# Message aggregation in three fp32r terms behind adjacency transposes and state parts, and the first norm's output of chunks 1 to 3 by ACT

## The reference

```python
x_conv = relu(h + x)                       # two convolutions, the second with 17 taps
s = x @ w_se.T + b_se                      # three position values of a node
A = exp(-dist(s, s)) * adj                 # (512, 512), weighed adjacency
msg = relu(x @ w_msg.T + b_msg)            # (512, 128)
x_nmp = einsum('nm,md->nd', A, msg)        # message aggregation
gi = concat(x_conv, x_nmp) @ w_ih.T + b_ih # gates of the inputs: r, z, n
gh = x @ w_hh.T + b_hh                     # gates of the state: r, z, n
r, z = sigmoid(gi_r + gh_r), sigmoid(gi_z + gh_z)
y = (1 - z) * tanh(gi_n + r * gh_n) + z * x
```

## Time and profile before

| | |
|---|---|
| median of 3 runs | 583.18 us (582.69 to 584.78) |
| profiled execution | 584.18 us, its span 582.4 us |
| PE busy | 560.3 us, 96% of the span |
| PE weight loads | 479.4 us, 82% |
| DVE | 476.7 us, 82% |
| ACT | 341.6 us, 59% |
| POOL | 120.8 us, 21% |
| mean granted TensorE clock | 0.988 |

### The profile page before, as it was taken

One profiled execution on the slowest core, in us unless ns is written; L12 is line 12 of the kernel. 1 busy time (PEld: TensorE's weight loads), 2 busy tenths in 40 slices (PEclk: granted clock), 3 DMA queues, 4 the chain that ended last, 5 costly groups with the idle time before them and its releaser, 6 DMA issues.

```text
span 582.4 us, 11740 instructions
## 1 busy us (share of the span) xinstructions
PE 560.3 (96%) x3583; PEld 479.4 (82%) x3583; DVE 476.7 (82%) x1798; ACT 341.6 (59%) x713; POOL 120.8 (21%) x143
## 2 busy tenths in 40 slices
PE   6888999999999999999999999999999999999894
PEld 6767897978888797979798888979797978889684
DVE  3898777888888887888888888888888988888665
ACT  2325555575675756665756667565667566575442
POOL 3311120213122130302121211203021213122110
PEclk9989999999999999999999999999999999999998
DMA  7890050030201103030303021020303030000000
GB/s 192 277 301 4 2 191 7 2 111 2 88 22 45 64 0 109 0 109 0 109 0 109 0 52 57 17 92 0 109 0 109 0 109 1 19 2 19 1 19 18
DMA packets 33300, 34.46 MB, mean 59 GB/s; under 512 B 1663, under 2 KB 22531, under 8 KB 33146
## 3 DMA queue, kind: packets, MB, share of 16 engines
q1 hardware_dynamic: 32986, 34.01, 18.6%
q10 hardware_dynamic: 288, 0.13, 0.1%
HBM read 29.74 MB, written 4.39 MB: 59 GB/s over the span
## 4 chain that ended last, share of the span: by engine, by line
PE 85%; DVE 1%; ACT 0%; issue 0%; POOLq 0%; POOL 0%; DVEq 0%
PE bank L260 14%; PE bank L262 14%; PE bank L261 13%; PE bank L1774 9%; PE pair L260 6%; PE pair L262 6%; PE pair L261 6%; PE bank L1608 4%; PE bank L1619 3%; PE bank L1710 2%; PE pair L1766 2%; PE pair L1698 2%; PE bank L1673 1%; PE bank L1716 1%; PE pair L1725 1%
## 5 line engine op out<-in xcount | busy, mean ns | idle before, releaser
L1147 POOL TENSOR_TENSOR rs<-ve,neg_half 128x4 f32<-128x4 f32 (+1 forms) x60 | 57.1, 952 | 279.0 <-DVE ve L1336 246.2
L260 PE MATMUL bank<-cd_hi,w_hi 128*128 128x256 f32 x272 | 77.5, 285 | 0.0
L261 PE MATMUL bank<-cd_lo,w_hi 128*128 128x256 f32 x272 | 76.7, 282 | 0.0
L262 PE MATMUL bank<-cd_hi,w_lo 128*128 128x256 f32 x272 | 76.5, 281 | 0.0
L1774 PE MATMUL bank<-P,msg 128*128 128x512 f32 x128 | 57.5, 592 | 0.0
L260 PE MATMUL pair<-aT_hi,x_hi 128*128 128x512 f32 x128 | 52.9, 413 | 0.1
L260 PEld LDWEIGHTS bank<-cd_hi,w_hi 128*128 128x128 f32 x272 | 51.3, 189 | 1.6
L261 PEld LDWEIGHTS bank<-cd_lo,w_hi 128*128 128x128 f32 x272 | 51.4, 189 | 1.4
L262 PEld LDWEIGHTS bank<-cd_hi,w_lo 128*128 128x128 f32 x272 | 51.3, 189 | 0.0
L262 PE MATMUL pair<-aT_hi,x_lo 128*128 128x512 f32 x128 | 50.4, 394 | 0.0
L261 PE MATMUL pair<-aT_lo,x_hi 128*128 128x512 f32 x128 | 50.3, 393 | 0.0
(11 more groups left out here) (367 smaller groups left out, 1522.3 us busy)
## 6 DMA issues: line engine op xcount, KB each, us to landing
adj_nat<-in_adj_dram SPq DMA_DIRECT2D x16, 1024.0 KB, 6.2
x_nat<-in_x_dram SPq DMA_DIRECT2D x16, 256.0 KB, 2.9
xt<-in_x_dram SPq DMA_DIRECT2D x3, 1280.0 KB, 11.4
out_dram<-y_out SPq DMA_DIRECT2D x15, 256.0 KB, 2.2
hw<-in_L_gnn_W_dram SPq DMA_DIRECT2D x2, 640.0 KB, 6.5
xt<-in_L_gnn_conv_w_dram SPq DMA_DIRECT2D x1, 1088.0 KB, 5.8
aT<-in_adj_dram SPq DMA_DIRECT2D x5, 96.0 KB
nat_ih<-in_L_gnn_w_ih_dram SPq DMA_DIRECT2D x1, 384.0 KB, 5.1
```

What stands on the lines that cost most here:

```text
L260: nc.tensor.matmul(o, lh, rh, start=start, stop=False)
L261: nc.tensor.matmul(o, lh, rl, start=False, stop=False)
L262: return nc.tensor.matmul(o, ll, rh, start=False, stop=stop)
L1147: g.tensor_tensor(rs[i][:, 0:n], ve[i][:, 0:n], neg_half[:, 0:n], ALU.pow).then_inc(po_rs[i], 1)
```

## The change

N becomes three fp32r terms. For that ACT rounds each weighed chunk (`P_hi`, four of 128x512) and the messages (`msg_hi`), POOL subtracts the rests of the four chunks (`P_lo`), DVE the rest of the messages (`msg_lo`). N's twelve products stand behind T0, T1, the state's parts of the gates z and r, and T2; the gates are taken in the order convolution parts of z, r, n, then message parts of z, r, n. In the turns without `new` the n gate goes behind the next turn's x3T. On ACT the exponentials 2 and 3 and the roundings go ahead of `y_out`; DVE's statistics of layer 3 go ahead of `nmp_lo` and the adjacency rests, and `aT_lo` of chunk 3 ahead of the sum of the n gate. The first norm's output of chunks 1 to 3 is written by ACT as `x1 * rs + fall`, with `fall` made by one small DVE instruction.

```diff
@@ -1174,6 +1180,11 @@
                         pool.wait_ge(dv_ve[3], V(0) + h)
                         g.tensor_tensor(rs[3][:, 2 * h:2 * h + 2], ve[3][:, 2 * h:2 * h + 2], neg_half[:, 0:2], ALU.pow
                                         ).then_inc(po_rs[3], 1)
+                if cur:
+                    for mc in range(NC):
+                        wait(pool, ac_Phi[mc], V(1))
+                        wait(pool, pe_N, V(0))
+                        g.tensor_tensor(P_lo[:, mc, :], P[:, mc, :], f(P_hi[:, mc, :]), ALU.subtract).then_inc(po_Plo[mc], 1)
                 if nxt:
                     inverse_root(V, 2, 2)
...
+
+                def round_weighed(mc):
+                    wait(act, dv_P[mc], V(1))
+                    wait(act, pe_N, V(0))
+                    s.activation(P_hi[:, mc, :], P[:, mc, :], ACT.Identity).then_inc(ac_Phi[mc], 1)
 
                 if cur:
...
@@ -1238,15 +1254,26 @@
                     wait(act, pe_P1, V(0))
                     s.activation(cd_hi[:, :, :], cd[:, :, :], ACT.Identity).then_inc(ac_cdh, 1)
                     wait(act, dv_s, V(1))
-                    wait(act, pe_N, V(0))
+                    wait(act, dv_msglo, V(0))
                     s.activation(msg_v[1], ms_half(ms_banks(nxt)[1]), ACT.Relu).then_inc(ac_msx, 1)
                     s.activation(msg_v[0], ms_half(ms_banks(nxt)[0]), ACT.Relu).then_inc(ac_msg, 1)
+                if nxt:
+                    wait(act, dv_fall, V(1))
+                    wait(act, dv_y3, V(1))
+                    wait(act, dv_xs[NC - 1], V(1))
+                    for c in range(1, NC):
+                        last = s.activation(x2[:, c, :], x1[:, c, :], ACT.Identity, bias=fall[:, c - 1:c], scale=rs[0][:, c:c + 1])
+                    last.then_inc(ac_x1r, 1)
+                if cur:
                     wait(act, pe_LR, V(1))
                     if not prev:
                         act.wait_ge(po_LR0, 1)
                     wait(act, pe_D[NC - 1], V(0))
                     s.activation(LR[0:KD, 0, :], SQ_BANK[0:KD, :], ACT.Identity)
                     s.activation(LR[0:KD, 1, :], SQ_BANK[GR:GR + KD, :], ACT.Identity).then_inc(ac_LR, 1)
+                    wait(act, ac_msg, V(1))
+                    wait(act, pe_N, V(0))
+                    s.activation(msg_hi[:, :], msg[:, :], ACT.Identity).then_inc(ac_msghi, 1)
                 if nxt:
                     wait(act, dv_f, V(2))
...
                     exponential(1)
+                if cur:
+                    round_weighed(0)
+                if nxt:
+                    wait(act, dv_e, V(2))
+                    wait(act, dv_dq, V(1))
+                    s.activation(pef[:, 0, :], ef[:, 0, :], ACT.Exp, bias=c12[:, 0:1]).then_inc(ac_pe, 1)
+                if nxt:
+                    wait(act, pe_agg2, V(2))
+                    s.activation(agg_sb[:, :], AG_BANK[:, :], ACT.Identity).then_inc(ac_agg2, 1)
+                if cur:
+                    exponential(2)
+                    exponential(3)
+                    round_weighed(1)
+                    round_weighed(2)
+                    round_weighed(3)
                 if prev and cur:
                     wait(act, po_shift, V(0))
                     wait(act, o_out, outs)
@@ -1270,16 +1312,7 @@
                         last = s.activation(y_out[:, c, :], X_BANK[:, ch(c)], ACT.Identity, bias=shift[:, c:c + 1],
                                             scale=rs[3][:, c:c + 1])
                     last.then_inc(ac_out, 1)
-                if nxt:
-                    wait(act, dv_e, V(2))
-                    wait(act, dv_dq, V(1))
-                    s.activation(pef[:, 0, :], ef[:, 0, :], ACT.Exp, bias=c12[:, 0:1]).then_inc(ac_pe, 1)
-                if nxt:
-                    wait(act, pe_agg2, V(2))
-                    s.activation(agg_sb[:, :], AG_BANK[:, :], ACT.Identity).then_inc(ac_agg2, 1)
-                if cur:
-                    exponential(2)
-                    exponential(3)
+                if cur:
                     wait(act, dv_conv, V(1))
                     wait(act, pe_gn, V(0))
...
                     wait(dve, ac_E[mc], V(1))
-                    wait(dve, pe_N, V(0))
+                    wait(dve, po_Plo[mc], V(0))
                     v.tensor_tensor(P[:, mc, :], AT_BANK[mc % 2][:, :], aT[par][:, mc, :], ALU.mult
                                     ).then_inc(dv_P[mc], 1)
...
                     v.scalar_tensor_tensor(gh, CV_BANK[:, :], 1.0, gh, ALU.add, ALU.mult).then_inc(dv_t0, 1)
+                def rest_of_state():
+                    wait(dve, ac_x3T, V(1))
+                    wait(dve, pe_r, V(0))
+                    v.tensor_tensor(x3T_lo[:, :], X_BANK[:, :], f(x3T_hi[:, :]), ALU.subtract).then_inc(dv_x3Tlo, 1)
+
+                if prev:
+                    if nxt:
+                        split_rest(3, 2)
+                    else:
+                        rest_of_state()
                     wait(dve, dv_t0, V(0))
                     wait(dve, pe_gn, V(0))
                     v.tensor_tensor(gh, SQ_BANK[:, :], gh, ALU.add).then_inc(dv_t, 1)
-                if nxt and prev:
-                    split_rest(3, 2)
-                if cur:
-                    wait(dve, ac_x3T, V(1))
-                    wait(dve, pe_r, V(0))
-                    v.tensor_tensor(x3T_lo[:, :], X_BANK[:, :], f(x3T_hi[:, :]), ALU.subtract).then_inc(dv_x3Tlo, 1)
+                if nxt and cur:
+                    rest_of_state()
                     if not prev:
...
@@ -1495,6 +1534,7 @@
                 if nxt:
 
                     hold(dve, po_rs[0], V(2))
+                    v.scalar_tensor_tensor(fall[:, :], mv[0][:, 1:NC, 0], -1.0, rs[0][:, 1:NC], ALU.mult, ALU.mult).then_inc(dv_fall, 1)
                     v.tensor_scalar(x1[:, 0, :], x1[:, 0, :], mv[0][:, 0, 0:1], rs[0][:, 0:1], ALU.subtract,
                                     ALU.mult).then_inc(dv_x1, 1)
                     wait(dve, dv_x1, V(2))
@@ -1508,13 +1548,8 @@
                     hold(dve, dv_mv[1], V(2))
                     v.tensor_scalar(ve[1][:, 0:1], mv[1][:, 0, 1:2], EPS, None, ALU.add).then_inc(dv_ve[1], 1)
 
-                    hold(dve, ac_xs[NC - 1], V(1))
-                    for c in range(1, NC):
-                        last = v.tensor_scalar(x2[:, c, :], x1[:, c, :], mv[0][:, c, 0:1], rs[0][:, c:c + 1],
-                                               ALU.subtract, ALU.mult)
-                    last.then_inc(dv_x1r, 1)
                 if nxt:
-                    hold(dve, dv_x1r, V(2))
+                    wait(dve, ac_x1r, V(1))
                     hold(dve, ac_pf, V(1))
                     for c in range(1, NC):
                         dot(1, c)
@@ -1559,6 +1594,10 @@
                     weigh(3)
                     wait(dve, pe_P1, V(1))
                     v.tensor_tensor(odd, HN_BANK[:, 0:HALF], base[:, 1, :], ALU.add).then_inc(dv_conv, 1)
+                if cur:
+                    wait(dve, ac_msghi, V(1))
+                    wait(dve, pe_N, V(0))
+                    v.tensor_tensor(msg_lo[:, :], msg[:, :], f(msg_hi[:, :]), ALU.subtract).then_inc(dv_msglo, 1)
                 if nxt:
 
...
@@ -1581,9 +1620,8 @@
                                            ALU.subtract).then_inc(dv_xclo, 1)
                 if nxt:
                     hold(dve, dv_y3, V(2))
-                    statistics(2, V, 2, lambda c: y3[:, c, :], EPS, rests_meanwhile)
-                else:
-                    rests_meanwhile()
+                    statistics(2, V, 2, lambda c: y3[:, c, :], EPS)
+                rests_meanwhile()
                 if nxt:
                     hold(dve, pe_x3T, V(1))
                     normalise(2, V, 2, lambda c: x3[:, c, :], lambda c: y3[:, c, :], dv_x3)
@@ -1672,6 +1710,8 @@
                     for c in range(NC):
                         last = t_.transpose(X_BANK[:, ch(c)], x3[:, c, :], ident[:, :])
                     last.then_inc(pe_x3T, 1)
+                if cur and not nxt:
+                    gate(SQ_BANK[:, :], of_inputs(2), pe_gn, 0)
                 if nxt:
                     wait(pe, ac_xhi, V(2))
...
                     last.then_inc(pe_out2, 1)
-                if cur:
-                    wait(pe, ac_msg, V(1))
-                    if prev:
-                        wait(pe, ac_out, V(0))
-                    for mc in range(NC):
-                        wait(pe, dv_P[mc], V(1))
-                        last = t_.matmul(X_BANK[:, :], msg[:, ch(mc)], P[:, mc, :], start=(mc == 0), stop=(mc == NC - 1))
-                    last.then_inc(pe_N, 1)
+                def gate_part(o, blk, hi, lo, start, stop):
+                    return three(pe, o, w_hi[:, blk, :], w_lo[:, blk, :], hi[:, :], lo[:, :], start, stop)
+
                 if new:
                     wait(pe, adj_in[par], dma(2))
                     for mc in range(2):
                         wait(pe, dv_P[mc + 2], V(1))
                         transpose_adjacency(mc)
```

(60 more changed lines are left out.)

4 lines of the change are left out of this document (3 added, 1 removed).

## The result

The changed kernel took a median of 587.50 us (585.47 to 590.99, nine runs), the kernel before 582.83 us in the runs beside them (581.86 to 584.78, nine runs). The ratio is 1.0074, with a 95% interval of 1.0048 to 1.0099: slower by 0.5 to 1.0%. 586.4 us had been predicted, with slower as the likeliest sign. The profiled execution of after took 587.50 us, its span 585.8, against 582.4 before.

The account below looks back on a forecast made before the run. PE was taken to bound turns 0 to 14, with a serial end behind turn 15's N. Terms 0 - 0.6 - 0.2 + 2.8 + 1.2 = +3.2 on 583.18 gave 586.4 us, range 580.5 to 592.5.

Parts of the forecast that it names:

- The sum: Whole kernel: 0 - 0.6 - 0.2 + 2.8 + 1.2 = +3.2 us.
- turns 0 to 13: Turns ahead of the end: no net change together, written as 0; a middle turn goes from 31.89 to 31.86 us.
- N itself: N on PE: twelve fp32r products take 2.83 us instead of 3.43, a gain of 0.60.
- From `out2` to N: Middle turn on PE: N starts 2.93 us behind `out2`, including a wait of 0.19 for T1.
- From N to conv1: Middle turn: DVE's queue delays `x3T_lo`; conv1 comes 8.27 us behind N's issue, 0.42 of it waiting.
- a gap of 0.3 to 0.5 there: Trace sign: PE waits 0.3 to 0.5 us behind `agg1` once per turn, conv1 started by `x3T_lo`.
- Turn 0: First turn, no earlier graph or `y_out`: the conv1 behind it comes 0.1 us later.
- Turn 14: From `out2`'s end, x3T comes at 8.65 and conv1 at 11.37 us: -0.5, and -0.1 for the gap.
- the sentence that contention adds nothing: DVE beside POOL's rests: `xc_lo` and statistics slip up to 1.6 us into slack of about 1.8, nothing added.
- The last N: Turn 15: N waits for `y_out` and runs 568.15 to 571.0 instead of ending at 568.24: +2.8 us.
- The clock: Around turn 15's N: PE idle 3.3 us ahead of it, then 1.2 GHz, costing 0 to 1.7, taken as 1.2.
- Rival C, POOL first: POOL's queued rests pass over `msg_lo` once; N starts 0.8 us late in 14 turns, +11.2, 597.6 us; chance 0.12.

Follow-up runs that it names:

- Order alone: The changed kernel with N back as four plain fp32 products in its new place, without its roundings and rests: 591.82 us, ratio 1.0128.
- `x_lo` early: The changed kernel with DVE making `x_lo` directly behind `nmp_lo`, no longer behind the norm of layer 3: 584.02 us, ratio 1.0014.
- combined: The changed kernel with `x_lo`, `y_out` and `msg_lo` moved early and N of turn 15 in fp32 without roundings and rests: 579.67 us, ratio 0.9932.
- N first: The changed kernel with N's three terms directly behind `out2`, ahead of the adjacency transposes and state parts of the gates: 623.33 us, one run.

## Why the prediction came out right, and which of its steps did not

**The sum** was +3.2 and the spans give +3.4. That it is closer than its terms is luck: turns 0 to 13 gave 1.06 that I had put at 0, and against that stand 0.60 at the start that is in no term, 0.30 less gained in turns 14 and 15 than forecast (0.50 for 0.8), and 0.36 more lost from the taps on (4.36 for 4.0). By the medians the loss is 4.7 us, by the ratio 4.3.

**N itself: right.** Twelve products took 2.89 (317.97 to 320.86 below) against 2.83, and the clean price is 0.62 a turn.

**From `out2` to N: right.** Timeline of PE in after, the turn of the earlier trace rows:

```profile
297.31 0.47 PE L264 MATMUL bank<-x3T_hi,w_hi 128*128 128x512 f32 x1
...
314.24 1.05 PE L1806 MATMUL pair<-plainT,agg_sb 128*128 128x130 f32 x8
315.23 1.16 PE L1646 MATMUL bank<-ident,adj_nat 128*128 128x128 f32 x8
...
317.97 0.48 PE L1830 MATMUL bank<-P_hi,msg_hi 128*128 128x512 f32 x1
...
320.86 0.39 PE L264 MATMUL bank<-xc_hi,w_hi 128*128 128x512 f32 x1
```

N starts 2.84 behind `out2`'s end (315.13, where the forecast was 2.93), and conv1 (329.06) 8.20 behind N's issue (8.27). The wait of T1 is 0.1 where 0.19 was forecast, and 0.1 stands ahead of T0, in no term. Conv1 to the end of `out2` is 17.82 (17.83). The turn is 31.75 where 31.86 was forecast, with the same parts in the same places. The forecast turn was even with before's mean of 31.847 (the turn of the earlier trace rows, 31.89, is one of its longer ones), so the measured mean of 31.768 gives the 1.0 us of turns 1 to 13.

**From N to conv1: right in its end, incomplete in its shape.** `x3T_lo` starts 7.41 behind N's issue (7.43 in the forecast) and ends 0.10 ahead of conv1 (0.15). The forecast had the whole wait of 0.42 behind `agg1`, and a gap of 0.3 to 0.5 there was one of its signs; it came as 0.17 there and 0.22 ahead of `agg1` (0.58 behind the transposes instead of 0.36), which begins 0.10 behind the end of `x_lo` in the same DVE queue, and the early `x_lo` took that second part away. "Order alone" and "`x_lo` early" show the step itself: order costs 0.54, and moving one DVE instruction returns 0.27.

**Turn 0: right.** By conv1 it gained 0.03, where 0.1 lost was written and rounded to 0.

**Turn 14: size off.** There conv1 came 11.66 behind `out2` where 11.37 was forecast (11.85 before), and x3T 9.05 where 8.65 was. The step that failed is the sentence that contention adds nothing. Timeline of DVE in after, turn 14:

```profile
538.39 1.37 DVE L1600 TENSOR_TENSOR msg_lo<-msg,msg_hi 128x512 fp32r<-128x512 f32 x1
...
540.15 0.76 DVE L1610 TENSOR_TENSOR dq<-dq,pef 128x4 f32<-128x4 f32 x1
...
545.48 1.11 DVE L1374 TENSOR_SCALAR x<-y,mv,rs 128x128 f32<-128x128 f32 x4 [0.57 <-POOL rs L1153]
```

`msg_lo` and a product of 128x4, both held beside POOL's rests, stand ahead of everything that leads to the statistics, and the norm then waits 0.57 for POOL's root. In the middle DVE has slack for this; in turn 14, which transposes no new adjacency, it is the path. Two runs show it. With `y_out` early alone N starts 0.48 sooner and x3T still comes at 9.05, so N's start is not what sets it. With `msg_lo` early as well `msg_lo` takes 0.68, the small product 0.38, and x3T comes at 8.08. How much of this 0.97 is the hold and how much is `msg_lo`'s own 0.68 in that place, no run separates.

**The last N: right, and for a cause one layer too thin.** The wait is 3.33 against 3.34. N takes 4.29 where its twelve products take 2.89 in the middle, so the clock cost 1.40 against 1.2; with what the cheaper products save the two rows are 4.19 against 4.0. But the prediction told the wait as one of `y_out`, and the runs showed two more behind it: with `y_out` and `msg_lo` both early 2.56 of the 4.19 stayed, waits for roundings and for POOL's rests, and with the last N not split on top of that (combined) all of it was gone. The clock was a guess that came true: the idle stretch of 1.95 in before was followed by 1.2 GHz, but in "N first" fourteen of 2.57 were not, so what decides it is open.

**Rival C, POOL first: refuted,** and with it the fear of 11 us. The instructions that write `msg_lo`, then `P_lo` and `dq`, in after (durations min/median/max in ns, first and last start), and behind them the timelines of POOL and DVE in the turn of the earlier trace rows:

```profile
L1600 DVE TENSOR_TENSOR msg_lo<-msg,msg_hi x16: 1345/1367/1377, 93.6 to 565.2; 128x512 fp32r<-128x512 f32 x16
```

```profile
L1187 POOL TENSOR_TENSOR P_lo<-P,P_hi x64: 1270/1452/1757, 89.7 to 567.7; 128x512 fp32r<-128x512 f32 x64
```

```profile
L1610 DVE TENSOR_TENSOR dq<-dq,pef x15: 764/778/784, 95.4 to 540.2; 128x4 f32<-128x4 f32 x15
```

```profile
315.46 4.24 POOL L1187 TENSOR_TENSOR P_lo<-P,P_hi 128x512 fp32r<-128x512 f32 x3 [1.23 <-ACT P_hi L1212]
```

```profile
315.93 1.37 DVE L1600 TENSOR_TENSOR msg_lo<-msg,msg_hi 128x512 fp32r<-128x512 f32 x1
```

`msg_lo` was held in 16 of 16 turns, to about twice its 0.69, and never passed over: it asks at 315.93 while POOL's three run from 315.46 on, and is done at 317.30, 0.67 before N. The first of the three ends at 316.75 and the second runs from 316.70 to 318.44, so DVE was served behind the first. Had it been passed over once, it would have ended near 318.7 (an estimate: 1.3 more of POOL and then its own 0.69).

With the rule cited from the Trainium skill, page "SBUF — State Buffer", section "Who interferes with whom", that the two engines exclude each other, the trace agrees: 16 of 16 `msg_lo` took 1.35 to 1.38 for 0.69, and 15 of 15 `dq` 0.76 to 0.78 for 0.16. It was right to let it widen the range and not move the forecast; where it took part in a loss was turn 14 and, behind `y_out`, the last N.

## What to carry to other kernels

Price a cheaper operation with its order held fixed: 0.62 us a turn were saved and 0.54 given back by the waits that its new place makes, so the change was only as good as the queue of the engine that became late. Look at the last iteration by itself. There nothing covers the extra roundings and rests, and leaving the last N as it was gave back 2.3 us in the traces and 3.0 by the ratios. When a profile names what ended a wait, look for the inputs that came just before it: moving `y_out` alone gained nothing measurable, since `msg_lo` was nearly as late.
